# A gated linear attention layer with experts on one core: the rounded copy of the right sides on VectorE, the exponents' parts in three steps, and a new order of jobs

## The reference

```
mixed = silu(causal_conv4(h @ Wqkv.T + bqkv))          # q, k, v
q = l2norm(q) * DK**-0.5 ; k = l2norm(k)
def step(state, (q_t, k_t, v_t, g_t, b_t)):
    state = state * exp(g_t)
    delta = (v_t - k_t @ state) * b_t
    state = state + outer(k_t, delta)
    return state, q_t @ state
core = core * rsqrt(mean(core**2) + 1e-6) * norm_w * silu(z)
out  = core @ Wout.T + bout
```

```
shared = x2 @ sw1.T * relu(x2 @ swg.T)**2 @ sw2.T
acc   += w_dense[:, e] * ((xl @ rw1[e].T) * relu(xl @ rwg[e].T)**2 @ rw2[e].T)   # e in 0..15
out    = shared + acc @ Wup.T
```

## Time and profile before

| | |
|---|---|
| median of 3 runs | 3316.34 us (3315.38 to 3320.57) |
| the profiled execution | 3309.96 us, its span 3308.2 us |
| busy over the span: PE, DVE, ACT, POOL | 92%, 79%, 74%, 69% |
| mean granted clock of PE | 0.976 |
| DMA queue q1, share of 16 engines | 16.1% |

### The profile page before, as it was taken

One profiled execution on the slowest core, in us unless ns is written; L12 is line 12 of the kernel. 1 busy time (PEld: TensorE's weight loads), 2 busy tenths in 40 slices (PEclk: granted clock), 3 DMA queues, 4 the chain that ended last, 5 costly groups with the idle time before them and its releaser, 6 DMA issues.

```text
span 3308.2 us, 74142 instructions
## 1 busy us (share of the span) xinstructions
PE 3040.9 (92%) x22560; PEld 2722.1 (82%) x22688; DVE 2625.7 (79%) x8462; ACT 2457.3 (74%) x5922; POOL 2275.8 (69%) x5380
## 2 busy tenths in 40 slices
PE   4999999999999999999999999999999999999996
PEld 3888888888888888888888888888888888888885
DVE  4788888888888888787878888888888878878874
ACT  3777777777777777777777777777787777787772
POOL 3777777767777777676767777777777767777670
PEclk8999999999999999999999999999999999999996
DMA  5111111111111111111111111111111111111110
GB/s 185 37 46 37 39 48 35 45 42 37 44 43 35 46 42 37 39 48 35 38 44 42 38 36 48 39 39 46 39 36 48 39 37 46 41 35 48 39 35 12
DMA packets 424102, 144.57 MB, mean 44 GB/s; under 512 B 211168, under 2 KB 421664, under 8 KB 423200
## 3 DMA queue, kind: packets, MB, share of 16 engines
q1 hardware_dynamic: 423712, 139.83, 16.1%
HBM read 93.11 MB, written 46.66 MB: 42 GB/s over the span
## 4 chain that ended last, share of the span: by engine, by line
POOL 38%; PE 22%; issue 17%; DMA 12%; ACT 7%; DVE 3%; POOLq 0%; SPq 0%; ACTq 0%; DVEq 0%
POOL Tp L1576 12%; POOL Tp L1583 8%; DMA DL<-Ln 7%; DMA Cb<-DL 5%; POOL Ln L1470 3%; ACT L839 3%; POOL Tp L1573 3%; PE bB L643 2%; POOL Tm L1585 2%; POOL Yb L1585 2%; POOL Yb L1600 2%; PE bF L475 2%; PE bX L522 2%; PE bQ L530 1%; PE bB L715 1%
## 5 line engine op out<-in xcount | busy, mean ns | idle before, releaser
L1148 DVE SCALAR_TENSOR_TENSOR Y<-bF,Cv,Y 128x127 f32<-128x127 f32 (+2 forms) x3072 | 853.3, 339 | 149.6 <-ACT Y L856 139.4
L475 PE MATMUL bF<-XnT,Wqkv 128*128 128x128 f32 x4096 | 561.0, 281 | 0.0
L475 PEld LDWEIGHTS bF<-XnT,Wqkv 128*128 128x128 f32 x4096 | 521.7, 194 | 13.5 <-issue 2.1
L928 ACT ACTIVATE XiT<-bXT 128x512 fp32r<-128x512 f32 x256 | 153.0, 598 | 436.2 <-PE bXT L559 436.2
L856 ACT ACTIVATE Y<-bF,Cv 128x128 f32<-128x128 f32 x1024 | 384.1, 458 | 77.7 <-PE bF L475 77.7
L1583 POOL TENSOR_TENSOR Tp<-Tp 32x64 f32<-32x64 f32 (+2 forms) x768 | 358.2, 466 | 60.2
L839 ACT ACT_TABLE_LOAD x257 | 329.7, 1283 | 5.3 <-PEq L1668 0.7
L1576 POOL TENSOR_TENSOR Tp<-Cb,Yb 32x64 f32<-32x64 f32 (+1 forms) x384 | 276.3, 719 | 30.1
L1576 POOL TENSOR_TENSOR Tp<-Yb,Tm 32x64 f32<-32x64 f32 (+1 forms) x384 | 275.9, 718 | 30.1
L572 PE MATMUL bX<-Xi,Qi 128*128 128x128 f32 x1536 | 285.1, 309 | 0.8 <-DVE Qi L1190 0.8
L1530 POOL TENSOR_TENSOR Ln<-Ln,Cf 128x512 f32<-128x512 f32 x128 | 163.8, 1280 | 173.8 <-DMA DL<-Ln 173.8
(11 more groups left out here) (228 smaller groups left out, 8645.1 us busy)
## 6 DMA issues: line engine op xcount, KB each, us to landing
DL<-Ln SPq DMA_DIRECT2D x128, 256.0 KB, 2.2
XiT<-DX SPq DMA_DIRECT2D x128, 256.0 KB, 2.8
Xi<-DX SPq DMA_DIRECT2D x128, 256.0 KB, 3.2
DX<-Yb SPq DMA_DIRECT2D x256, 32.0 KB, 1.9
Xf<-x SPq DMA_DIRECT2D x32, 128.0 KB, 2.9
Wqkv<-wqkv SPq DMA_DIRECT2D x4, 1024.0 KB, 17.4
Cb<-DL SPq DMA_DIRECT2D x128, 32.0 KB, 1.9
Xr<-x SPq DMA_DIRECT2D x32, 128.0 KB, 3.1
```

Of the source, the lines that this page charges most:

```text
L475: last = mm(bank[:, i, :], Wqkv[:, k, c:c + P], XnT[:, k, :], start=(k == 0), stop=(k == KT - 1))
L1148: last = stt(y, bank[:, i, 0:P - shift], Cv[:, g * TILES + tile, n:n + 1], y, ALU.mult, ALU.add)
```

## The change

There are three parts.

1. The rounded copy `Rr` of `R` moves from ACT (`activation` with Copy) to DVE (`tensor_copy`), right behind `right_side`. Its wait for `zs_full` is dropped.
2. POOL's `exponents` makes the three bf16 parts in four instructions instead of five: the second part comes directly from the subtraction, rounded by its output type, beside the same subtraction in fp32 (`HGf`, now half as large), and the third directly from the next. Three dependent steps are left. The sum for `HG`'s third quarter moves behind them.
3. The jobs of an item are in a new order on PE, ACT, DVE and POOL. SP's order stays. Each engine still does the same jobs per item.

```
-            def rounded_r(w):
-                act.wait_ge(sem["r_done"], at("r_done", w))
-                act.wait_ge(sem["zs_full"], at("zs_full", ahead(w, -1)))
-                op(Rr[:, :, :], R[:, :, :], ACT.Copy).then_inc(sem["rr_done"], 1)
...
+            def rounded_r(w):
+                dve.wait_ge(sem["r_done"], at("r_done", w))
+                nc.vector.tensor_copy(Rr[:, :, :], R[:, :, :]).then_inc(sem["rr_done"], 1)
...
                 tt(Parts[:, 0:n], HG[:, 0:n], one, ALU.mult).then_inc(sem["parts_done"], 1)
+                pool.wait_ge(sem["parts_done"], at("parts_done", f, 1))
+                tt(Parts[:, n:2 * n], HG[:, 0:n], Parts[:, 0:n], ALU.subtract).then_inc(sem["parts_done"], 1)
+                tt(HGf[:, :], HG[:, 0:n], Parts[:, 0:n], ALU.subtract).then_inc(sem["parts_done"], 1)
+                pool.wait_ge(sem["parts_done"], at("parts_done", f, 3))
+                tt(Parts[:, 2 * n:3 * n], HGf[:, :], Parts[:, n:2 * n], ALU.subtract).then_inc(sem["parts_done"], 1)
                 tt(HG[:, 2 * GH:3 * GH], HG[:, GH:2 * GH], HG[:, 3 * GH:4 * GH], ALU.add).then_inc(sem["hg_done"], 1)
-                pool.wait_ge(sem["parts_done"], at("parts_done", f, 1))
-                tt(HGf[:, 0, :], HG[:, 0:n], Parts[:, 0:n], ALU.subtract).then_inc(sem["parts_done"], 1)
-                pool.wait_ge(sem["parts_done"], at("parts_done", f, 2))
-                tt(Parts[:, n:2 * n], HGf[:, 0, :], one, ALU.mult).then_inc(sem["parts_done"], 1)
-                pool.wait_ge(sem["parts_done"], at("parts_done", f, 3))
-                tt(HGf[:, 1, :], HGf[:, 0, :], Parts[:, n:2 * n], ALU.subtract).then_inc(sem["parts_done"], 1)
-                pool.wait_ge(sem["parts_done"], at("parts_done", f, 4))
-                tt(Parts[:, 2 * n:3 * n], HGf[:, 1, :], one, ALU.mult).then_inc(sem["parts_done"], 1)
```

More of the change, by code:

```diff
@@ L742, in item @@
                 new, front, invert, state, post, e, c = [s in stages for s in "afispec"]
+                if c and g == 1:
+                    chunk_front(t + 1, "ba")
                 if state:
                     ks(w)
[L745 to L750, removed]
                 if front:
@@ L766, in item @@
                     vtr(f)
+                if post:
+                    core_t(u)
+                if front:
+                    exponents(f)
+                if new:
+                    proj(a, 1, 1)
                 if e and g == 1:
                     experts(t - 1, "hT", 0)
-                if front:
-                    exponents(f)
                 if state:
@@ L803, in item @@
                     experts(t - 1, "D", 3)
+                if invert:
+                    invert_x(v, 1)
                 if e and g == 2:
                     experts(t - 1, "G", 2, a if new else (chunks - 1, GROUPS - 1))
[L806 to L810, removed]
                 if new:
                     z_proj(a, 0)
+                    z_proj(a, 1)
                 if c and g == 0:
@@ L816, in item @@
                     experts(t - 1, "laT", 0)
+                if invert:
+                    invert_q(v, 2)
+                if state:
+                    new_state(w)
                 if e and g == 2:
                     experts(t - 1, "D", 2)
[L819 to L822, removed]
                 if e and g == 3:
@@ L1033, in item @@
                 new, front, invert, state, post, e, c = [s in stages for s in "afispec"]
+                if front:
+                    key_norm(f)
+                if new:
+                    last_tap(a, 0)
+                if front:
+                    keys(f)
                 if state:
                     query_state(w)
[L1036 to L1043, removed]
                 if front:
@@ L1069, in item @@
                     corrected(w)
+                if c and g == 0:
+                    chunk_front(t + 1, "norm")
                 if invert:
@@ L1089, in item @@
                     activated(a)
+                if e and g == 0:
+                    experts(t - 1, "norm2", 0)
+                if c and g == 0:
+                    chunk_front(t + 1, "ba")
                 if e and g == 3:
                     experts(t - 1, "ffo", 0)
[L1092 to L1093 removed]
+                if state:
+                    out_norm(w)
+                if front:
+                    rounded_l(f)
                 if invert:
                     inverse(v, 2)
[L1096 to L1099 removed]
             run(act, item)
@@ L1369, in item @@
                 new, front, invert, state, post, e, c = [s in stages for s in "afispec"]
+                if front:
+                    squares(f)
+                if e and g == 2:
+                    experts(t - 1, "D", 0)
                 if state:
                     right_side(w)
-                if e and g == 2:
-                    experts(t - 1, "D", 0)
-                if front:
-                    squares(f)
+                    rounded_r(w)
+                if e and g == 1:
+                    experts(t - 1, "hn", 0)
                 if post:
                     gated(u)
+                if front:
+                    products(f)
+                if new:
+                    ended(a)
                 if c and g == 1:
                     chunk_front(t + 1, "sp")
-                if new:
-                    ended(a)
-                if e and g == 1:
-                    experts(t - 1, "hn", 0)
-                if front:
-                    products(f)
                 if new:
@@ L1420, in item @@
                     taps(a, 1, 0)
+                    tails_out(a, 1)
                 if e and g == 2:
```

100 lines of the change are left out of this document (45 added, 55 removed).

## The result

The changed kernel takes 3274.1 us (median of 4 runs) and the kernel before 3315.9 us in the same measurement: the ratio is 0.9879, 95% interval 0.9848 to 0.9911, so 1.2% faster. Measured again beside the last experiments the ratio was 0.9845 (0.982 to 0.987). The profiled execution took 3271.6 us, its span is 3269.8 us, and its mean clock 0.973 (before 0.976).

What follows compares the result with a forecast made beforehand. It took PE's own work and PE's waits, mainly for DVE in group 0, as close limits. Terms summed to -1.35 us per chunk, times 31 -42 us: 3268, plus 6.4 for the median, 3274 us; range 3200 to 3345.

Steps and rivals of the forecast that it cites:

- case A: Whole kernel: some waits go and smaller ones come, 3274 us, between 3245 and 3305; chance 0.50.
- wait at L510: PE's wait at `ktr` for DVE's `Sse` goes entirely, as `squares` precedes `right_side`: -1.4 us per chunk.
- parts and `Kn`: PE's waits for POOL's parts and ACT's `PartsT`: 1.2 of 1.9 us stay, -0.7 per chunk, bounds -1.9 and 0.
- wait at L559: PE's wait at `invert_xt` for DVE's `Qi`: +0.2 us per chunk over its 1.4, between -0.5 and +1.2.
- `z_proj`: PE reaches it earlier in group 0 and waits for `first_tokens`' second half: +0.4 us per chunk (0.2 to 0.9).
- `La`: PE's transpose of `La` in group 3 comes earlier and must wait: +0.45 us per chunk (0.3 to 0.6).
- `Sq`: PE's earlier `ss` may wait for ACT's `Sq`, above all in group 1: +0.3 us per chunk (0 to 0.9).
- clock: Group 0's clock falls behind two idle stretches, costing 0.9 us per chunk; two thirds come back: -0.6 (0 to -0.9).
- The late one behind POOL: At PE's `parts_t`, once POOL is out of the way, ACT is late next, through `keys` and the `PartsT` copy.
- rival D: DVE blocked by POOL in group 0, up to 1.1 us each, clock falling in all chunks: 3404 us; chance 0.17.
- The first row that I took for the copy: DVE's cast of 1792 columns, 1.095 us, used to estimate the rounded copy at 0.35 us with start-up.
- the first term: `squares` ahead of `right_side` on DVE removes PE's whole wait at `ktr`: -1.4 us per chunk.

Runs made afterwards that it cites:

- the repeat: The changed kernel itself, unaltered, timed once more beside the other experiments: 3260.3 us, ratio 0.9845 to the kernel before.
- `squares` back: The changed kernel with DVE's `squares` again behind `right_side` and the rounded copy: 3258.0 us, ratio 0.9838 to the kernel before.
- before + fill: The kernel before with PE's out projection in group 0 moved ahead of the first `invert_xt`: 3287.8 us, ratio 0.9927.
- both filled versions: The changed kernel with group 0's out projection ahead of `invert_xt`, 3236.5 us; the same with `keys` (group 1) and third `invert_q` (group 3) moved earlier, 3232.1 us.
- copy on ACT: The changed kernel with the rounded copy on ACT again, directly behind `key_norm`: 3270.5 us, ratio 0.9869 to the kernel before.
- `mask_q` first: The changed kernel with DVE's first-level `mask_q` ahead of `first_tokens` in all groups: 3314.4 us, ratio 1.0012 to the kernel before.
- `decay_keys` back: The changed kernel with POOL's `decay_keys` again behind `before_first`: 3304.5 us, ratio 0.9984 to the kernel before.

## Why the prediction was right, and where not

It gave 3274 us and 3274.1 was measured, in the forecast case A. That the two agree to 0.1 us is luck: the repeat gained 51 us where this measurement gave 42, and below, large errors of single terms cancel. Per chunk, measured as the difference of the waits in both kernels over 30 chunks:

| term | predicted | measured |
|---|---|---|
| wait at L510 | -1.4 | (0.8 - 42.6) / 30 = -1.4 |
| parts and `Kn` (L516, L530 on ACT) | -0.7 | (33.1 - 56.7) / 30 = -0.8 |
| wait at L559 | +0.2 | (48.5 - 42.0) / 30 = +0.2 |
| `z_proj` (L486) | +0.4 | 0.0 |
| `La` (L732) | +0.45 | +0.5 |
| `Sq` (L503) | +0.3 | (12.0 - 1.7) / 30 = +0.3 |
| clock | -0.6 | about +0.5 (below) |
| L547, L530 on issue, L715 | none | +0.25 - 0.25 + 0.1 = +0.1 |
| sum | -1.35 | -0.6, against 98.5 - 99.6 = -1.1 |

The rows miss the measured difference by 0.5. By the windows over steady running PE's idle time fell by 1.3 us per chunk (6.2 to 4.9) and its busy time rose by 0.2 (2897.97 / 31.0 = 93.4 to 93.6), which makes -1.1. So the rows, which list only the named waits, miss some 0.2 of idle time, and 0.3 of busy time went somewhere else; no run shows where.

**The late one behind POOL** was named rightly: ACT (`Kn`, `PartsT`), with 1.1 of 1.9 us left. The run with five-step parts shows that this gain needs no shorter parts. But it is not the order's alone: the copy alone already took these two waits from 56.7 to 28.6 us.

**The wait at L559** came out right by errors that cancel. The step "takes `left_over` and ACT's late `Y` out and adds the copy 0.35: 9.15" failed: DVE's chain takes 10.0 us, as the copy takes 0.43, and `gated`, beside `decay_keys`, 0.8 us more than at its best; rival D named that block, and the sum left it out. With that chain my own sum gives 1.24 + 0.1 + 1.4 = 2.7 us, less what holds PE up before; 1.6 was measured, so PE was held up by 1.1 where I took 0.4 to 0.8. `first_tokens`, for which I allowed up to 1.1, took 0.58 for 0.36. And the 1.4 that I set the wait against was no value of group 0: it had the waits of group 1 in it. In group 0 alone the wait grew by (48.5 - 34.8) / 30 = 0.5 us, and group 1's 0.2 went.

The first row that I took for the copy, 0.61 ns a column, was too low; 0.43 lies between the bounds. Four of the 128 copies took over 0.6 us. The longest, in the last items, met a product of POOL that had begun 0.06 us before it:

```profile
3188.99 1.03 POOL L1532 TENSOR_TENSOR Kd<-Kn,Sc 128x512 f32<-128x512 f32 x1
...
3189.05 1.26 DVE L1206 CAST Rr<-R 128x512 fp32r<-128x512 f32 x1
```

It ended 0.3 us behind `Kd`, so it did most of its work after it. By the Trainium skill ("SBUF — State Buffer", section "SBUF: two separate sides") a two-port copy on DVE locks GpSimd out and is locked out in turn; the trace agrees for the second half of that, with 1.26 for 0.43, and it was rare since `Kd` starts behind the copy.

That `first_tokens` would lie beside `Ln` or `AT` in every group was wrong for group 1. There it was blocked in 25 of 30 chunks before (over 0.9 us) and takes 0.16 now; in groups 2 and 3 it takes 0.6 to 0.7 instead of 0.17 (means).

**`z_proj`** does not wait: the front of the item got later on PE by the longer L559 and the slow out projections, so `first_tokens`' second half was in time. With the gap filled, the predicted wait appears: 15.2 us, 0.5 per chunk.

**The clock** is the term that failed, by its sign. The step "the first of the two idle stretches goes, the second stays or grows: I take two thirds back" took the number of stretches for what counts. Slow groups were to fall from 8 to under 4; they rose to 22, far above the 8 that its text gave as the limit, so by its own sign it is wrong here. The one stretch that was left had grown from 1.2 to 1.6 us. The item's length, from `ks` to `ks`, by the starts in PE's timeline (mean, number of chunks in brackets):

| kernel | group 0 not slow | slow | next group behind each |
|---|---|---|---|
| before | 22.8 (22) | 25.6 (8) | 27.5, 27.5 |
| changed | 23.1 (8) | 25.3 (22) | 26.3, 25.7 |
| repeat | 23.1 (8) | 25.2 (22) | 26.0, 25.8 |

A slow group cost 2.8 us before. In the changed kernel it costs 2.2, and the next group is 0.6 shorter: 1.6 (2.1 and 0.2, so 1.9, in the repeat). Per chunk 8 x 2.8 / 30 = 0.75 became 22 x 1.6 / 30 = 1.2, in the repeat 22 x 1.9 / 30 = 1.4: +0.4 to +0.6, where -0.6 was predicted. My 3.4 us came from one window of 8 us and was above the mean of the 8 slow groups, 2.8.

**D** did not come: of its two blocks `gated`'s was there with 0.8 us, the copy's was rare. (Its sum also holds 1.1 us for blocks where its text puts 2.2 on the wait.) Its other half, the low clock, did come in 22 of 30 chunks; its price was half of what D took. As the text wanted for its forecast, PE's idle time is between 4 and 6 us, and DVE is busy 85%, ACT 73% (84 and 72 foreseen).

What the first term gave is not what the change gave. With `squares` back, the wait at L510 is back and the time no worse. Nor is the gain in the shorter parts or in the engine of the copy. It lies in the rest of the order, with the copy at a place where it isn't late and `decay_keys` ahead of `before_first`. Counted from `ks` to `ks`, groups 1 to 3 got shorter by 1.6, 0.7 and 0.1 us and group 0 longer by 1.2. Of both the 1.6 and the 1.2, 0.4 us is only a job of PE (`ba`, L657) that stood behind group 1's `ks` and now stands ahead of it. Most of the other 0.8 in group 0 is the clock: at full clock it takes 23.1 us for 22.8, and with `ba` set apart about as long as before, though 1.2 us of wait at L510 are gone from it. Which single move in the order carries the 2.0 us of groups 1 to 3 wasn't tried.

## What to carry to other kernels

- Taking away a wait of PE that one engine's chain sets can only move the wait to that chain's next result, and two short waits can become one long one, behind which the clock falls more often. Fill the gap with work of PE that is ready, as the out projection here; that gave 27 to 38 us on top of a reordering worth 42 to 51, most of it by the clock, and 24 us without it.
- Test an order with the work where the order needs it. Here the order alone gave +2.2%, the copy alone -0.3%, and both without the shorter parts -1.4%.
- In a program that rests on short operations of DVE between long products of POOL, look at each exchange of neighbours for what is blocked and for who only shares the semaphore: two such exchanges cost 1.1 to 1.7% each.

## What the runs showed that I had not expected

How often the clock falls in group 0 goes, by and large, with the mean length of the wait at L559 there (counted by item in the timeline, since the rows of some kernels mix in short waits of group 1), and not with the sum of PE's waits:

| kernel | mean wait at L559 in group 0 | slow groups 0 of 30 |
|---|---|---|
| before + fill | none | 0 |
| both filled versions | 0.43, 0.44 (in 21 chunks) | 1, 0 |
| copy on ACT | 0.87 | 8 |
| order alone | 0.88 | 0 (of 29) |
| `squares` back | 0.94 | 7 |
| copy alone | 1.02 | 7 |
| `mask_q` first | 1.16 | 1 (of 29) |
| before | 1.16 | 8 |
| parts alone | 1.17 | 7 |
| changed, repeat | 1.62, 1.56 | 22, 22 |
| `decay_keys` back, five-step parts | 1.66, 1.66 | 24 (of 29), 22 |

Two kernels do not fit, the order alone and `mask_q` first: they wait 0.9 and 1.2 us and are slow there never and once; why stays open. That the idle stretch brings the clock down, rather than both coming from the same late DVE, is argued from the filled versions, which took the stretch away and the slow groups with it.
